# A graph-and-experts kernel: GpSimd pauses for landing behind every third block of gathers in place of every second, with the next slot looked up ahead of the pause

## What is computed

```python
edge_index = jnp.stack([src, dst])          # 100000 edges, sorted by dst
x = x + L0_gnn(layernorm(x), relvectors, GRU weights, src, dst, edge_type)
x = x + L0_ffn(layernorm(x))                # shared MLP and 2 of 4 small experts
x = x + L1_gnn(layernorm(x), W, b, edge_index)
x = x + L1_ffn(layernorm(x))                # 2 of 8 experts, hidden size 1024

# L0_gnn                                     # L1_gnn
msg = h[edge_src] + relvectors[edge_rel]     # xt = x @ W.T + b
red = segment_sum(msg, edge_dst)             # out = segment_sum(xt[src], tgt)
return gru_cell(red, h, ...)                 # return out / (deg + 1)
```

## Time and profile before

| | |
|---|---|
| median of 3 runs | 3773.45 us |
| lowest, highest | 3770.12, 3796.68 us |
| the profiled execution's own time | 3769.46 us |
| its span, first to last instruction | 3767.9 us |
| mean granted TensorE clock | 0.739 |
| layer 0, gathers first to last start | 141.7 to 1587.2 us |
| layer 1, gathers first to last start | 1656.9 to 2956.6 us |

### The profile page before, as it was taken

How to read it: one execution, slowest core, us unless ns; L and a number is a source line. 1 busy time by engine, 2 the same in 40 slices (tenths; PEclk the granted TensorE clock), 3 DMA queues, 4 the chain that set the end, 5 groups by cost and what they waited for, 6 DMA issues and landing times. The chain is left out here.

```text
span 3767.9 us, 54160 instructions
## 1 busy us (share of the span) xinstructions
PE 2407.2 (64%) x13318; PEld 1817.1 (48%) x13319; DVE 1524.1 (40%) x3970; ACT 778.7 (21%) x1414; POOL 1832.3 (49%) x2044
## 2 busy tenths in 40 slices
PE   1288888878776754346666555444432499999992
PEld 1155555555543442234444333222221299999992
DVE  6444444444442332034444433232221255545545
ACT  1223222222211210020100000000000054444541
POOL 0354444455555555425555555555555344444441
PEclk7588888888877765566666665555655599999996
DMA  5222222222222222222322322222222212112215
GB/s 138 85 81 62 68 66 64 70 72 73 84 84 78 84 79 85 71 66 84 90 84 84 90 83 84 79 84 81 85 84 81 70 63 87 43 66 64 64 45 216
DMA packets 157828, 303.02 MB, mean 80 GB/s; under 512 B 47365, under 2 KB 91816, under 8 KB 157752
## 3 DMA queue, kind: packets, MB, share of 16 engines
q0 software_dynamic: 85984, 234.74, 21.4%
q1 hardware_dynamic: 40876, 36.11, 3.1%
q10 hardware_dynamic: 30892, 31.40, 2.5%
HBM read 261.73 MB, written 40.39 MB: 80 GB/s over the span
## 5 line engine op out<-in xcount | busy, mean ns | idle before, releaser
L745 POOL DMA_INDIRECT rows<-table,srcT x1568 | 1531.5, 977 | 1225.8 <-issue 979.9
L812 PE MATMUL bank<-rows,onehot 128*128 x3904 | 763.4, 354 | 912.5 <-POOLq L736 696.2
L812 PEld LDWEIGHTS bank<-rows,onehot 128*128 x3904 | 449.5, 115 | 1212.8 <-issue 1060.1
L773 DVE SCALAR_TENSOR_TENSOR onehot<-iota_row,tbase,dstT 128x512 f16 x488 | 366.8, 752 | 798.4 <-issue 532.5
L1774 PE MATMUL bank<-xe_high,W_high 128*128 128x256 f32 x864 | 252.3, 292 | 30.2 <-DVE xe_low L1852 29.9
L1824 ACT ACTIVATE hid<-bank,b 128x256 f32<-128x256 f32 x432 | 181.2, 471 | 345.6 <-PE bank L1776 344.6
L1775 PE MATMUL bank<-xe_low,W_high 128*128 128x256 f32 x864 | 250.3, 290 | 0.0
L1776 PE MATMUL bank<-xe_high,W_low 128*128 128x256 f32 x864 | 250.0, 289 | 0.0
L1774 PE MATMUL bank<-W_high,hid_high 128*128 128x256 f32 x864 | 248.3, 287 | 0.0
L1860 DVE TENSOR_TENSOR hid_low<-hid,hid_high 128x512 fp32r<-128x512 f32 x216 | 149.6, 693 | 234.3 <-ACT hid_high L1828 230.7
L1776 PE MATMUL bank<-W_high,hid_low 128*128 128x256 f32 x864 | 243.9, 282 | 0.0
(11 more groups left out here) (338 smaller groups left out, 3645.3 us busy)
## 6 DMA issues: line engine op xcount, KB each, us to landing
rows<-table,srcT POOLq DMA_INDIRECT x1568
W<-in_L_ffn_W_dram SPq DMA_DIRECT2D x14, 1024.0 KB
y<-results ACTq DMA_DIRECT2D x12, 1024.0 KB, 9.8
x_res<-in_x_dram SPq DMA_DIRECT2D x1, 6144.0 KB, 42.6
out_dram<-x_res SPq DMA_DIRECT2D x12, 512.0 KB
table<-part ACTq DMA_DIRECT2D x11, 512.0 KB
normal<-xn ACTq DMA_DIRECT2D x11, 512.0 KB
table<-part SPq DMA_DIRECT2D x6, 512.0 KB, 2.9
```

What stands on the lines that cost most here:

```text
L745: nc.gpsimd.indirect_dma_start(out=rows[:, k % (M * U), 0:ROW], out_offset=None, in_=q.table, in_offset=bass.IndirectOffsetOnAxis(srcT[:, ...
L773: last = nc.vector.scalar_tensor_tensor(onehot[:, ds(slot, U), :], iota_row[:, :].unsqueeze(1).to_broadcast([P, U, P]), base, dstT[:, ds(k ...
L812: last = nc.tensor.matmul(acc[:, 0:cols], hot, ring_rows[:, ds(row0 + (s * q.pitch + at), cols)], start=False, stop=False, skip_group_chec ...
```

## The change

`pool_chunks` now reports at other places. Blocks go in threes. The first of three is reported in the middle of the second, the second in the middle of the third, and the third behind its own gathers: the pause is behind blocks 2, 5, 8, ..., 194, and behind the last block, 195. The lookup and the wait for a slot become a function, `free(i)`, which is called once ahead of the loop and then for block i + 1 behind the gathers of block i, ahead of the pause. Block, gather and semaphore counts stay as they are.

```diff
+                def free(i):
                     pool.wait_ge(q.used, pool.value_load(frees[0:1, i:i + 1], min_val=1, max_val=NT * (PASS + 1) + MH))
                     settled(pool)
+
+                free(0)
+                for i in range(BLOCKS):
+                    stops = i % 3 == 2 or i == BLOCKS - 1
                     for s in range(U):
-                        if i % 2 == 1 and s == U // 2:
+                        if i % 3 > 0 and s == U // 2:
                             ready(i - 1, 1)
...
-                    if i % 2 == 1:
+                    if i + 1 < BLOCKS:
+                        free(i + 1)
+                    if stops:
                         ready(i, 1 if i < BLOCKS - 1 else 1 + PASS - BLOCKS)
```

More of the change, by code:

```diff
@@ L736, in ready @@
                     pool.sem_inc(q.rows_ready, blocks)
-                for i in range(BLOCKS):
+                def free(i):
                     pool.wait_ge(q.used, pool.value_load(frees[0:1, i:i + 1], min_val=1, max_val=NT * (PASS + 1) + MH))
                     settled(pool)
+                free(0)
+                for i in range(BLOCKS):
+                    stops = i % 3 == 2 or i == BLOCKS - 1
                     for s in range(U):
-                        if i % 2 == 1 and s == U // 2:
+                        if i % 3 > 0 and s == U // 2:
                             ready(i - 1, 1)
```

## The result

The changed kernel took 3732.45 us (median of 4 runs, 3729.61 to 3746.63), the kernel before beside it 3778.67 us (median of 4). The ratio is 0.988, with a 95% interval of 0.983 to 0.993: 1.2% faster, 46 us, where 193 us (5.1%) were forecast. The profiled execution took 3731.25 us (span 3729.7).

The account below looks back on a forecast made before the run. POOL was taken to bound layer 0's end and layer 1, PE the rest. Savings of 132 (layer 1), 60 and 5 (layer 0), less 4 of losses, made 193 us: 3769.5 to 3576 us, range 3550 to 3625.

Parts of the forecast that it names:

- What bounds each stage: Layer 0 paced by PE until about 1096 us, by POOL to 1588; layer 1 by POOL to 2957; experts by PE.
- the price of a pause: POOL's gap between gathers at a pause: 1.84 us landing plus 0.81 us to the next gather, 2.65 us, from 3.24.
- 132 us: Layer 1's saving, from POOL's idle time between gathers falling from 537.5 to 405.7 us.
- the slower gathers: Gathers slowed by VectorE as POOL's busy share rises: 2 us more, within small losses of 4 us.
- With that cover I put it at 0: Block i's report stands behind the wait for slot i+1; PE still has six signalled blocks, so cost 0.
- In between PE is the bound and nothing is gained: Layer 0 between its start and about 1096 us: PE sets the pace, so a faster POOL saves nothing.
- the 60 + 5 us: Layer 0's savings: 60 us at its POOL-paced end, 1528 in place of 1588, and 5 us at its start.
- The size of layer 0's gain: Layer 0's whole saving: 60 us at its end and 5 us of PE's 11.0 us wait at its start.
- R1: PE becomes the bound in layer 1's early windows, losing 49 us of the gain: 3625 us; chance 0.13, full or part.
- R2: The lookup ahead of the pause hides nothing and a pause stays 3.24 us: 3629 us; chance 0.06.
- R3: Landing gets later when twelve gathers instead of eight go without a pause; gain gone at 0.82 us later; chance 0.06.
- The 4.9 us of "issue": PE's idle time ahead of L812 in layer 1's early windows, counted with 6.7 us as slack against a 6.0 us gain.

Follow-up runs that it names:

- ahead_only: Against the changed kernel, the pause is behind every second block again, with the lookup still ahead of it; ratio 0.978 to the kernel before.
- before_b: The kernel before, unedited, traced again on chip 12; 3723.22 us, ratio 1.001.
- gap_e: Changed kernel with 2.5 us without a gather behind the eighth gather of each three blocks in layer 0, on chip 5; ratio 0.973 to the kernel before.
- layer1_only: Changed kernel with the schedule of before put back in layer 0, so the new one is in layer 1 alone, on chip 11; ratio 0.973 to the kernel before.
- after_b: The changed kernel, unedited, run again on chip 12; 3509.80 us, ratio 0.943 to the kernel before.
- no_pause: Against the changed kernel, no pause but the last, each block reported in the middle of the next, on chip 9; ratio 0.885 to the kernel before.

## Why the prediction was wrong, by its own steps

- *What bounds each stage*: right. So was the price of a pause: 1.84 + 0.81 = 2.65 us forecast, 2.60 us the median (2.59 in the row above), and POOL's idle time between layer 1's gathers (405.2 against 405.7 us). Layer 1 saved 122 of 132 us on the chip of the result, and 138 on chip 12. The 10 us are the slower gathers, for which the sum had 2 us: their busy time rose by 11.
- *"With that cover I put it at 0"*, the report behind the wait for a slot: right by ahead_only, which has that order and lost nothing.
- *"In between PE is the bound and nothing is gained"*: the step that failed. It let the middle of layer 0 only stay as it was. On the chip of the result it got longer. At the start of window 40 (of 49) the changed kernel was 121 us behind before (1173.9 against 1053.2), and the 60 + 5 us forecast for the ends of the layer could only take back a part: it ended 85 us behind. The cost was a term that the sum didn't have: what a longer row of gathers does to the sequencers of other engines. Over the layer PE was busy for 49 us more and idle for 70 us more in the dense steps (ahead of L916 41 us in place of 16, ahead of L1016 44 in place of 22), and its idle time ahead of the blocks' matmuls fell by 34 us, where it fell by 73 on chip 12. That the longer busy time comes from the lower clock, and the waits in the dense steps from VectorE's own stalls, was not tried apart.
- *The size of layer 0's gain* was then right where nothing stalls: 75 us against 65.
- *R1* didn't come: POOL waited for PE 18.2 us in layer 1, 19.6 before; on chip 12 it was 15.5 against 30.5. *R2* is out: the pause shrank by the lookup. *R3* named the right place to look, twelve gathers in a row, and the wrong victim: not the landing was late (1.8 us still, mid-block gaps 0.30), but PE and DVE.
- *What the trace of before held*: 62 and 50 stalls, nearly all from the sixth gather of a row of eight on, so the kernel before was losing time to them as well. On its chip layer 0 took 1446 us, on chip 12 1398. The views hold them in "L812 <- issue", 69.5 us up to 1095.9, but little of it is stalls (11 us over the whole layer lie under one): 10.8 us are the wait for the layer's first report, and before_b, without a stall, has 45.4 us over the whole layer in gaps of at most 0.8. I took all of it for PE's own overhead and never looked at the register instructions. The 4.9 us of "issue" in the earlier trace rows, counted as slack, were slack: PE's sequencer has no record from 1765.4 to 1770.3 us, and L736's event is at 1770.3. It was one more wait for POOL's report whose update is missing from the trace. A long gap with no cause shown can be either; the sequencer's own records tell which.

Left open: what holds the sequencers. The runs show when (from the fifth gather of a row on, mostly from the seventh), for how long (0.70 us), on which engines (TensorE, VectorE, and GpSimd in gap_e) and that it differs by chip: chips 5 and 11 and the chip of the result have it, 3, 8, 9 and 12 don't. Of the first kind the kernel before took 3779 to 3805 us, of the second 3718 to 3723. Every execution told of here was recorded, with the granted clock; whether one that isn't recorded has the stalls is open too, and the lost records make it the first thing to try.

## What to carry to other kernels

A pause on one engine can be what keeps others going, at least while an execution is recorded: when a change lets an engine issue longer rows of DMAs, ask not only what waits for those DMAs, but what else shares the chip with their making. In the stage where another engine is the bound, price a speed-up of the idle engine as a possible loss, and look for idle time put down to "issue" that is longer than the loop's usual gap. Then read what the engine's sequencer did in that gap: held register instructions are one thing, a wait whose signal the trace has lost is another. Where records are lost, compare all idle time ahead of an instruction and not its named parts. Before a theory built on one chip is believed, run the pair on a second: here one kernel change is worth 1.2% on one chip and 5.7% on the other, and each was measured to half a per cent.

## What the runs showed of the hardware

- Register instructions of TensorE's and VectorE's sequencers, 0.01 to 0.2 us as a rule, were held for 0.70 us (some for 1.38) in recorded executions while GpSimd issued gathers back to back. Of the 481 in the changed kernel 479 began at the fifth gather of a row or later; on chip 11 a few came earlier (8 of 398 in layer1_only). Chips 5 and 11 did so, and the one of the result, whose number isn't known; chips 3, 8, 9 and 12 did not.
- The traces of those same chips, and no others, lack updates of semaphores: 23780 are recorded in before and 19251 in the changed kernel, 38490 and 38481 in before_b and after_b.
- A lookup of a register's value on GpSimd costs nothing ahead of a landing and 0.62 us behind it: the median pause of layer 1 is 3.22 us in the kernel before and 2.58 in ahead_only, which was forecast to save 58 us over layer 1's 97 pauses and saved 61 on chip 11.
- A gather's descriptors took 971 to 988 ns on average in layer 1 of each kernel, with pauses or without. With the gap of 0.30 us that is some 1.29 us each: 784 x 1.29 = 1011 us, and no_pause's layer 1 took 1017.
